# First layer of a two-layer graph network: tile sums moved to another PSUM bank, lagging two groups instead of three, and issued after the third edge layer

## What is computed

```python
# first layer, per edge e
h = gelu(edge_attr_8 @ Wfc1 / sqrt(8)); h = gelu(h @ Wfc2 / 8); w = h @ Wfc3 / 8     # 192 weights
gs, gv = f_s[src], f_v[src]                    # gathered rows of the projected node table
mid0 = w0 * gs * y0;           mid1 = w3 * sum_c(gv * y1)
mid2 = (w1 * gs)[:, :, None] * y1[:, None, :];  mid3 = w2[:, :, None] * gv * y0
# summed over the edges with the same dst, then a linear map per node
x = layernorm(x + res(segment_sum(mid, dst)))
# second layer: same shape of work, edges gathered by dst and scattered (added) by src
```

## Time and profile before

| what | us |
|---|---|
| runs without the profiler, median of 3 | 2656.18 |
| fastest and slowest of them | 2644.06, 2663.58 |
| profiled execution, span from first to last instruction | 3060.6 |
| profiled, first gather to last gather issued (first layer) | 51.6 to 1462.0 |
| profiled, first scatter to last scatter issued (second layer) | 1523.6 to 3008.6 |

### The profile page before, as it was taken

The page is one execution under the profiler, slowest core; times in us unless marked ns, Lnnn a source line. Parts: engine busy times, 40 slices in busy tenths (PEclk is TensorE's granted clock), DMA queues, the critical chain, the costliest instruction groups (busy, mean ns, idle before and its releaser), DMA issues.

```text
span 3060.6 us, 78767 instructions
## 1 busy us (share of the span) xinstructions
PE 2639.6 (86%) x24556; PEld 1983.6 (65%) x24556; DVE 1645.1 (54%) x4537; ACT 984.7 (32%) x2591; POOL 2008.3 (66%) x1630
## 2 busy tenths in 40 slices
PE   7667777886768877876799999999999999999997
PEld 4334444443434444443588888888888888888883
DVE  3446434443444444444466666666666666666664
ACT  2212212221221221221244444444444444444442
POOL 4555554555555555555188888888888888888885
PEclk5566656657676566566699999999999999999998
DMA  6233332332233233332388888888888888888877
GB/s 193 59 96 93 86 89 77 89 93 79 82 93 83 81 95 82 86 94 80 83 140 141 141 141 140 141 141 139 141 141 140 140 140 142 140 140 140 141 136 176
DMA packets 392755, 356.11 MB, mean 116 GB/s; under 512 B 60112, under 2 KB 343440, under 8 KB 392368
## 3 DMA queue, kind: packets, MB, share of 16 engines
q0 software_dynamic: 150528, 141.40, 32.0%
q1 hardware_dynamic: 237552, 208.10, 24.3%
q10 hardware_dynamic: 4544, 4.93, 0.5%
HBM read 246.44 MB, written 133.44 MB: 124 GB/s over the span
## 4 chain that ended last, share of the span: by engine, by line
PE 77%; issue 9%; another core or an unknown queue 8%; DVE 2%; ACT 2%; DMA 1%; POOL 1%; SPq 0%; ACTq 0%; DVEq 0%; POOLq 0%
PE ps_o L1051 11%; PE ps_w L1039 10%; PE ps_d L1060 8%; PE ps_o L1049 8%; PE ps_w L901 7%; PE ps_pg L842 6%; PE ps_x L1073 6%; PE ps_h L894 6%; PE ps_h L888 3%; PE ps_x L1013 3%; PE ps_pg L857 2%; PE ps_pg L851 1%; PE ps_pg L854 1%; PE ps_nd L917 1%
## 5 line engine op out<-in xcount | busy, mean ns | idle before, releaser
L623 POOL DMA_INDIRECT tab<-summed,sidx x784 | 1223.2, 1560 | 284.4 <-issue 230.8
L605 POOL DMA_INDIRECT gat<-f,gidx x784 | 753.4, 961 | 694.7 <-DVE feats L1358 384.9
L1498 DVE TENSOR_TENSOR prod<-ps_w,xg 128x768 f32<-128x768 f32 x392 | 375.4, 958 | 266.3 <-PE ps_w L1039 252.7
L1051 PE MATMUL ps_o<-ro_v,prod 128*128 128x96 f32 x3136 | 479.1, 275 | 0.0
L842 PE MATMUL ps_pg<-feats,sel 128*32 128x320 f32 x1568 | 225.9, 661 | 265.7 <-issue 265.5
L1051 PEld LDWEIGHTS ps_o<-ro_v,prod 128*128 128x128 f32 x3136 | 414.1, 192 | 0.0
L797 ACT ACTIVATE xg<-ps_x 128x768 f32<-128x768 f32 x392 | 296.4, 808 | 341.3 <-PE ps_x L1073 340.3
L1039 PE MATMUL ps_w<-hid,wf 64*128 64x128 f32 x4704 | 368.7, 289 | 2.0 <-ACT hid L798 2.0
L1049 PE MATMUL ps_o<-ro_s,prod 96*128 96x96 f32 x1568 | 327.5, 291 | 19.0 <-DVE msg L1509 4.8
L1039 PEld LDWEIGHTS ps_w<-hid,wf 64*128 64x128 f32 x4704 | 293.5, 187 | 70.2 <-issue 44.6
L1060 PE MATMUL ps_d<-msg,same 128*128 128x193 f32 x1568 | 332.3, 334 | 0.7 <-ACT summed L816 0.7
(11 more groups left out here) (262 smaller groups left out, 3451.0 us busy)
## 6 DMA issues: line engine op xcount, KB each, us to landing
xt<-in_src_rows SPq DMA_DIRECT2D x196, 256.0 KB
xt<-feat SPq DMA_DIRECT2D x784, 36.0 KB
xt<-in_ea SPq DMA_DIRECT2D x196, 128.0 KB
feat<-xt SPq DMA_DIRECT2D x25, 576.0 KB
hot_dst<-in_dst_rows SPq DMA_DIRECT2D x98, 128.0 KB
gat<-f,gidx POOLq DMA_INDIRECT x784
hot_dir<-sh_rows SPq DMA_DIRECT2D x98, 128.0 KB
xt<-hot_dst SPq DMA_DIRECT2D x196, 64.0 KB
```

Source lines behind the costliest of these rows:

```text
L605: pool.indirect_dma_start(out=gat[:, r % 4, k, :], out_offset=None, in_=t["f0"], in_offset=bass.IndirectOffsetOnAxis(ap=gidx[:, r // 4, at ...
L623: pool.indirect_dma_start(out=t["tabs"][into[k]], out_offset=bass.IndirectOffsetOnAxis(ap=sidx[:, r, k:k + 1], axis=0), in_=summed[:, r, k ...
L1051: last = pe.matmul(ps_o[:, k, 96 + 64 * c:192 + 64 * c], prod[:, ur % 2, k, 1 + c, :], ro_v[:, c, :], start=True, stop=True)
L1498: dve.tensor_tensor(prod[:, r % 2, :, :, :].rearrange("p k c e -> p k (c e)"), ps_w4[:, :, 0:3 * P], xg[:, r // 2, r % 2 * 2:r % 2 * 2 + 2 ...
```

## The change

- `ps_p` moves from the bank `ps_pg` to `ps_hy[:, 128:448]`, the bank that holds one half of layer1's output. `ps_g` stays in `ps_pg`.
- The waits follow the banks: layer1(s) now also waits for collect(s-3), the tile sums of step s also wait for the first gelu of step s (`g1_done`), and no longer for `acc_done`.
- The lag of the tile sums, collect and window sums is SUM_LAG = 2 groups (it was 3). `add_window` stays at 2.
- On PE, layer3(s-1) is issued before the tile sums, not after layer2.
- On DVE, positions(s) and add_window(s-2) are issued before products(s). `place` has four buffers (it had two).
- The tail of the loop is one step shorter on PE (`split_steps(pe, NGRP, SUM_LAG, ...)`).

```diff
+SUM_LAG = 2
-            place = sb(c2, "place", [P, 2, 4, WIN])
+            place = sb(c2, "place", [P, 4, 4, WIN])
-            ps_p = ps_pg[:, 0:FEAT]
-            ps_g = [ps_pg[:, FEAT + 4 * WIN * i:FEAT + 4 * WIN * (i + 1)] for i in range(2)]
+            ps_p = ps_hy[:, P:P + FEAT]
+            ps_g = [ps_pg[:, 4 * WIN * i:4 * WIN * (i + 1)] for i in range(2)]
# ACT, gelus
-                    v, _, vr = lagged(u, j, r, 3, 16)
+                    v, _, vr = lagged(u, j, r, SUM_LAG, 16)
# PE, layer1
                     pe.wait_ge(ea8_in[r], 16 * (j + 1))
+                    since(pe, part_done, u - SUM_LAG)
                     since(pe, g2_done, u)
# PE, step
                             layer1(s, r, j)
-                        u, _, ur = lagged(s, j, r, 3, 2)
+                        v, _, vr = lagged(s, j, r, 1, 2)
+                        if runs(v, NGRP):
+                            layer3(v, vr)
+                        u, _, ur = lagged(s, j, r, SUM_LAG, 2)
                         if runs(u, NGRP):
+                            pe.wait_ge(g1_done, min(s + 1, NGRP))
                             since(pe, part_done, u)
-                            since(pe, acc_done, u)
                             pe.wait_ge(sel_ready, u + 1)
                             pe.wait_ge(prod_done, u + 1)
                             tile_sums(pe, ur, part_ready)
                         if runs(s, NGRP):
                             layer2(s, r)
-                        v, _, vr = lagged(s, j, r, 1, 2)
-                        if runs(v, NGRP):
-                            layer3(v, vr)
                         if runs(u, NGRP):
                             pe.wait_ge(part_done, u + 1)
                             pe.wait_ge(place_ready, u + 1)
                             since(pe, acc_done, u)
-                            window_sums(pe, parts[:, ur, :], place[:, ur, :, :], ur, agg_done)
+                            window_sums(pe, parts[:, ur, :], place[:, u % 4, :, :], ur, agg_done)
-                    split_steps(pe, NGRP, 3, step, head=NGRP)
+                    split_steps(pe, NGRP, SUM_LAG, step, head=NGRP)
# DVE, step
                             select(s, r % 2, pad_off[:, bass.ds(s * G, G)], s + 1)
-                            products(s, j, r)
-                        u, _, ur = lagged(s, j, r, 2, 4)
+                            since(dve, agg_done, s - 3)
+                            positions(r, slot_rel[:, bass.ds(s, 1)])
+                        u, _, ur = lagged(s, j, r, SUM_LAG, 4)
                         if runs(u, NGRP):
...
                             add_window(ur % 2, base)
                         if runs(s, NGRP):
-                            positions(r % 2, slot_rel[:, bass.ds(s, 1)])
+                            products(s, j, r)
```

More of the change, by code:

```diff
@@ L775, in _ @@
                 steps(act, NGRP, gelus, NGRP, 16)
-                for u in range(NGRP - 3, NGRP):
+                for u in range(NGRP - SUM_LAG, NGRP):
                     act.wait_ge(part_done, u)
@@ L980, in step @@
                         layer1(u, r, j)
-                        if not isinstance(u, int) or u >= 3:
+                        if not isinstance(u, int) or u >= SUM_LAG:
                             pe.sem_inc(part_ready, 1)
@@ L994, in general @@
                     steps(pe, NGRP, step, 4, 2)
-                    for _ in range(2):
+                    for _ in range(SUM_LAG - 1):
                         pe.sem_inc(part_ready, 1)
@@ L1420, in fast @@
                     chained[0] = 0
-                    split_steps(dve, NGRP, 2, step, 4, head=NGRP)
+                    split_steps(dve, NGRP, SUM_LAG, step, 4, head=NGRP)
                     for v in range(LOOPED[-1] + 1, NT):
```

## The result

The changed kernel takes 2618.24 us (median of 5 runs, 2615.82 to 2620.82), where the kernel before took 2644.80 in the 5 runs beside it (2641.28 to 2663.58): 0.9902 of the time, with an interval of 0.9873 to 0.9931. That is 26.6 us less, or 1.0%. The forecast was 15 us less. (The 2656.18 that it started from is the median of three of these five runs.)

What follows compares the result with a forecast made beforehand. The prediction took POOL to bound the runs, with a floor of 2629.0 us: 2656.2 - 3.3 (tail) - 12 (loop) = 2641 us, 0.6% less. Its own range was 2629 to 2653, the 8-in-10 range 2580 to 2668.

Steps and rivals of the forecast that it cites:

- rival 2: Recording slows POOL too: its instructions are 0.05 us shorter in the runs, giving 2590 us; chance 0.30.
- I take these waits to belong to recording, and not to the runs.: First-layer waits on another core or an unknown queue, 17.7% of the chain, were taken as absent from the runs.
- The floor of 2629.0: Whole kernel held by POOL: 51.6 to the first gather, 978.8 for gathers, 1598.6 after the last, 2629.0 us.
- The hidden term, 12 of 0 to 23.9: First layer: the loop over PE and DVE gives back 0 to 23.9 us in the runs; the middle, 12, was taken.
- Rival 1: Hidden altogether: POOL has the lead, the excess isn't the loop, only the tail is gained, 2653 us; chance 0.20.
- POOL as the bound: POOL's gathers, 1.25 us each, allow a group of four no more often than every 5.00 us.
- At 1.2 GHz 5.60, at 2.4 GHz 3.12: First layer: PE's period per group in us after the change, by its clock, where the loop took 6.04 and 4.23.
- Bank and wait on the add: the loop is cut.: First layer: tile sums no longer wait for the add, saving 0.44 us a group at 1.2 GHz, 1.11 at 2.4.
- Order on DVE: cost 0.: First layer: add_window and positions ahead of products cost 0, bounds 0 to 0.5 us a step.
- The tail, -3.3: After the last products, one of two remaining rounds runs beside the products: -3.3 us, bounds -6.5 and 0.
- Rival 3: First layer: PE waits for gathers, drops to 1.2 GHz and stays there, 90 us slower, 2743 us; chance 0.12.
- The profiled span, 3060.6 to about 2937: In the profiled execution the span falls to about 2937 us if the foreign waits stay: 120 from groups, 3.3 from tail.

Runs made afterwards that it cites:

- experiment 1: The kernel before run again unchanged, for another trace of it: 2639.95 us, ratio 1.0002, span 2648.3 us.
- the second trace: The profile of the unchanged kernel before, recorded again in experiment 1: span 2648.3 us, where the first trace had 3060.6.
- experiment 8: Kernels with three gathers a group instead of four: before 2587.8 us, changed 2521.38, bank and layer3 ahead at lag 3 2540.77, layer3 ahead alone 2445.56.
- experiment 5: The changed kernel with DVE's old order, products, then the add, then positions: 2631.85 us, ratio 0.9976 to the kernel before.
- the second trace of after: Another profile of the changed kernel, unaltered: span 2618.7 us, where its first trace had 2615.9.
- experiment 7: The kernel before with only layer3 issued ahead of the tile sums: 2626.67 us, ratio 0.9937; beside it the changed kernel again, 2621.13 us, 0.9917.
- experiment 6: The kernel before with the bank moved and layer3 issued ahead, lag 3 and DVE's order as before: 2616.12 us, ratio 0.9902.

## Why the prediction was right, and where it wasn't

**The outcome.** 2618.2 lies in the range, the sign was right, and 1.0% less is right at the edge of what the forecast called distinguishable. The likeliest case had 15 us of the 26.6. Its own range, 2629 to 2653, was missed by 11 us on the fast side. The wide range holds the result only because it made room for rival 2, whose reason turned out wrong, so that part is luck.

**"I take these waits to belong to recording, and not to the runs."** Half right. They weren't in the runs. But they don't belong to recording: experiment 1 records the same kernel without them. So every number taken from that trace as "what it takes here" was open to doubt, and the next step used some.

**The floor of 2629.0.** This is the step that failed, a size and not the mechanism. Its terms for the start (51.6) and the gathers (978.8) hold. The third, 1598.6 for all after the last gather, was swollen by the same odd execution; the second trace has 2648.3 - 1072.8 = 1575.5, of which the scatters are 1470.1 instead of 1485.0 and the turnover 51.9 instead of 61.6. The floor is 53 + 979 + 1575.5 = 2607, 22 us lower, and the changed kernel was measured below the "floor" of the forecast. With it the per-group pace of the runs was mis-sized too: not 5.14 but 1019.8 / 195.75 = 5.21.

**The hidden term, 12 of 0 to 23.9.** Mis-sized through that floor. The gathers' excess over 978.8 was 41.0 us before and is 18.3 after, so the cut gave back 22.7, about 55% of it. Rival 2 had assumed 60% of a larger excess, for another reason (recording slows POOL), and that reason is wrong: gathers have a median of 946 ns in an ordinary execution, and the recorded executions take no longer than the others. Rival 1 (hidden altogether, 2653) is wrong as well.

**POOL as the bound.** Right for the changed kernel with four gathers: the chain has the gathers in front, products wait for gathers, POOL waits 17.6 us for products, and the gathers come every 5.09 us where POOL alone needs 5.00. For the kernel before it holds in part. With a quarter of the gathers gone it gains only 1.7%, 5.21 to 4.87 us a group, so the loop over PE and DVE stood close behind POOL, and the same change is worth 66 us there (experiment 8).

**"At 1.2 GHz 5.60, at 2.4 GHz 3.12".** 5.60 was met exactly, and 3.22 stands against 3.12, 0.1 too little, half of it because half of layer1's 0.73 was taken where it measures 0.42 (510.23 - 509.81). The old loop of 6.04 and 4.23 was met in the second trace as well, 6.04 and 4.24.

**"Bank and wait on the add: the loop is cut."** The mechanism, the loop through the shared bank, was right, but the cut was put down to the wrong edit. The bank alone changes nothing (0.9999), and layer3 ahead alone cuts the loop with the bank still shared (0.9937). The forecast called layer3 the cover of the new gelu wait, at cost 0. That was right, and without it the changed kernel is 2.3% slower than before (1.0232); but the same 0.86 or 1.59 us also cover the old wait, and for that the forecast gave the order nothing.

**"Order on DVE: cost 0."** No cost shows (0.9902 with the new order and lag 2, 0.9902 with the old one and lag 3), so the number stands. What the text didn't see is that lag 2 without it would cost: 0.6 to 0.7% (experiment 5).

**The tail, -3.3.** From the start of the last products' second part to the end of the last add: 7.25 us before (1079.64 to 1086.89 in the second trace) and 3.63 after:

```profile
1055.73 1.01 DVE L1360 TENSOR_TENSOR feats<-ps_w,gat 128x384 f32<-128x384 f32 x2
...
1059.19 0.17 DVE L1368 TENSOR_TENSOR acc_b<-acc_b,ps_pg 128x24 f32 x1
```

So -3.6, or -2.8 by the second trace of after, on either side of -3.3. But the size agrees by luck in part. These traces have PE at different clocks at this end (0.73 before, 1.00 and 0.50 after), and among the three traces at 0.50 the bank takes 2.5 us off and the rest, lag 2 among it, 1.1 (experiment 7), where the forecast gave all of it to the lag. The turnover as a whole fell by 7.4 and 6.8; experiment 6, at lag 3, has 45.7 and so nearly all of that.

**Rival 3, PE loses its clock.** In kind it came: the mean clock of the first layer fell from 0.83 to 0.79 (groups wholly at 1.2 GHz rose from 19 of 158 to 29 of 160). But the forecast's reason was longer idle time on PE, and that didn't come: idle time in 200 to 1000 us fell from 124.1 to 86.8 us. And since the gathers hold the pace, PE's period of 5.60 us against POOL's 5.00 seems to have cost less than the shorter periods gave; no run separates the two. The price of 90 us wasn't paid.

**The profiled span, 3060.6 to about 2937.** Wrong, 2615.9: the base was the odd execution, and the foreign waits, which the forecast expected to stay, are gone.

No version with four gathers is shown to beat the changed kernel: bank and layer3 at lag 3 has the same ratio, 0.9902.

## What to carry to other kernels

Where the span of a profile is far from the time of the runs, take another profile of the same kernel before reading any term out of it; a floor made of pieces of such a trace inherits its stalls, here 22 us, nearly the whole gain of 26.6. A wait between two engines can be hidden by what stands between its producer and its consumer as well as removed by another buffer: three moved lines of issue order opened this loop and gave two thirds to three quarters of the gain, where the other bank alone only traded the wait for the add for a wait for the gelu. And an edit in a chain of edits is known only when run alone: of four parts here one carries most, one adds little, and one (lag 2) mainly needs another to repair it.

## What the runs showed of the hardware that wasn't expected

One execution of the kernel before took a span of 3060.6 us with waits of up to 13.9 us in its first layer that no queue of the trace explains; 71 further ones of the same program were all at or under 2660.6 us, and no other trace has such waits in its chain. What it waited for isn't settled.

PE's clock doesn't follow its busy share. In 200 to 1000 us of the kernels with three gathers, PE was busy for 757.05 us (95%) at a mean clock of 0.79 with bank and layer3 moved, and for 739.74 us (92%) at 0.95 with layer3 alone; the second layer of each is at 0.99 to 1.00 with 98% or more. The same tile sums are busy for 0.74 us at 2.4 GHz and 1.29 at 1.2, so a busy share rises when the clock falls and isn't independent of it. The two kernels differ in the bank and in which wait ahead of tile sums ends last. That one of these is the cause of the clock wasn't shown: the pair was run once, on one chip, in four timed executions each (2527.4 to 2558.4 and 2443.1 to 2450.2 us, so it isn't the chance of one execution). It would take the same kernel with idle work put in ahead of tile sums to tell. For four gathers the same pair shows 0.79 and 0.80, no difference.
